# A decoder of 13 blocks on one core: value products moved ahead in the attentions, and a sampling block rewritten

## The reference

```
q, k, v = x @ Wq + bq, ctx @ Wk + bk, ctx @ Wv + bv      # ctx is x itself in self-attention
att = softmax(q @ k.T * scale, masked)                   # 128 x 128 for each sample and head
y   = x + (att @ v) @ Wo + bo
```

```
off  = x @ w_off + b_off                     # two numbers a point
attw = softmax(x @ w_attw + b_attw)          # over the 4 points of a head
ix   = ((clip(off[..., 0], 0, 1) + 1) * L - 1) / 2       # a place between two context rows
hy   = a factor of the other coordinate, 0 to 1
sampled = v[x0] * (1 - frac(ix)) + v[x0 + 1] * frac(ix)  # linear interpolation, v = ctx @ w_value + b_value
out = x + (sum over points of attw * hy * sampled) @ w_out + b_out
```

## Time and profile before

| | |
|---|---|
| runs | 2893.71, 2899.68, 2900.45 us; median 2899.68 |
| profiled execution | 2894.97 us, its span 2893.3 us |
| mean granted clock of PE | 0.934 |
| PE busy | 2543.5 us, 88% of the span |
| DVE busy | 1754.3 us, 61% |
| ACT busy | 1333.5 us, 46% |
| POOL busy | 809.0 us, 28% |

### The profile page before, as it was taken

How to read it: one execution, slowest core, us unless ns; L and a number is a source line. 1 busy time by engine, 2 the same in 40 slices (tenths; PEclk the granted TensorE clock), 3 DMA queues, 4 the chain that set the end, 5 groups by cost and what they waited for, 6 DMA issues and landing times. The chain is left out here.

```text
span 2893.3 us, 48158 instructions
## 1 busy us (share of the span) xinstructions
PE 2543.5 (88%) x15973; PEld 1864.1 (64%) x15973; DVE 1754.3 (61%) x4475; ACT 1333.5 (46%) x3461; POOL 809.0 (28%) x627
## 2 busy tenths in 40 slices
PE   4998989989778789599998998987969889869997
PEld 2666756766555446477776776756965566449996
DVE  7876886589788644344444657874336488434443
ACT  2333664255687513444443445753432388323342
POOL 5533430045100044122211224741110044132222
PEclk8999999999877699799999999988989999989999
DMA  9001000000200144200001002033120120531110
GB/s 320 11 0 50 14 12 9 1 16 1 63 8 1 23 116 118 102 1 1 1 1 41 23 1 74 2 127 105 38 90 6 39 62 5 186 120 50 54 50 26
DMA packets 152054, 142.45 MB, mean 49 GB/s; under 512 B 59948, under 2 KB 136770, under 8 KB 151428
## 3 DMA queue, kind: packets, MB, share of 16 engines
q1 hardware_dynamic: 139668, 110.61, 13.2%
q0 software_dynamic: 10560, 27.19, 2.7%
q10 hardware_dynamic: 1584, 1.57, 0.2%
HBM read 98.14 MB, written 43.02 MB: 49 GB/s over the span
## 5 line engine op out<-in xcount | busy, mean ns | idle before, releaser
L970 POOL TENSOR_TENSOR room<-room 128x1024 f32<-128x1024 f32 x144 | 273.8, 1902 | 414.4 <-DVE room L903 414.3
L1445 PE MATMUL l3f_out<-room,Y 128*128 x624 | 141.0, 380 | 0.0
L897 DVE TENSOR_REDUCE room<-room 128x8 f32<-128x1024 f32 (+1 forms) x144 | 140.0, 972 | 0.8 <-ACT room L1048 0.8
L970 POOL TENSOR_TENSOR room<-room,Y 128x1024 f32<-128x1024 f32 x32 | 60.7, 1896 | 232.6 <-DVE Y L903 232.6
L1445 PEld LDWEIGHTS l3f_out<-room,Y 128*128 128x128 f32 x624 | 115.8, 190 | 14.0
L2488 POOL DMA_INDIRECT sorted_rows<-room,l1f_place_i x32 | 31.0, 967 | 277.7 <-DVE l1f_place_i L2199 268.2
L1046 ACT ACTIVATE room<-l2a_scores,Y 128x128 f32<-128x128 f32 x256 | 71.0, 379 | 75.2 <-DVE Y L889 75.2
L1046 ACT ACTIVATE room<-l1a_scores,room 128x128 f32<-128x128 f32 x256 | 71.4, 386 | 59.6 <-DVE room L889 59.6
L1046 ACT ACTIVATE room<-l0x_scores,room 128x128 f32<-128x128 f32 x256 | 70.5, 384 | 59.0 <-DVE room L889 59.0
L614 PE MATMUL l2a_proj<-room 128*128 128x256 f32 x384 | 93.9, 388 | 0.0
L1747 DVE SCALAR_TENSOR_TENSOR Y<-Y,vecs 128x256 f32<-128x256 f32 x39 | 18.9, 484 | 114.3 <-DMA Y<-out,l3f_dest 114.2
(11 more groups left out here) (832 smaller groups left out, 7062.1 us busy)
## 6 DMA issues: line engine op xcount, KB each, us to landing
sorted_rows<-head SPq DMA_DIRECT2D x1, 16640.0 KB, 57.9
room<-in_L_ffn_w SPq DMA_DIRECT2D x16, 1024.0 KB, 12.9
room<-in_L_ffn_W SPq DMA_DIRECT2D x16, 1024.0 KB, 12.1
Y<-sorted_rows SPq DMA_DIRECT2D x62, 130.0 KB, 2.1
room<-in_ctx SPq DMA_DIRECT2D x24, 256.0 KB, 2.8
room<-sorted_rows SPq DMA_DIRECT2D x39, 130.0 KB, 2.1
room<-results SPq DMA_DIRECT2D x8, 512.0 KB, 7.2
room<-in_L_ffn_routed_w SPq DMA_DIRECT2D x4, 512.0 KB
```

Of the source, the lines that this page charges most:

```text
L897: dve.tensor_reduce(rsum[:, u % 2, 0:SUMMED], p[:, u % (TURN + 1), 0:SUMMED, :], AX.X, ALU.add)
L970: pool.tensor_tensor(p[:, u % (TURN + 1), :, :], p[:, u % (TURN + 1), :, :], rinv[:, u % (TURN + 1), :].unsqueeze(2).to_broadcast([P, HEAD ...
L1445: mm = pe.matmul(obank[n % 2][:, 0:D], hT[:, n % 2, f, :], chip.room[:, bass.ds(at + (SLOT // 2 + f * D), D)], start=(f == 0), stop=(f == ...
```

## The change

Two parts. **In `attention_block`**, so in six blocks, PE issues `values(t-VALUES)` directly behind `score(t)`, ahead of every projection and of the turn of that step; and ACT's copy of the value products moves from behind the evictions of place 1 to directly behind the first exponentials. DVE and POOL keep their order. **`deform_block`** is rewritten. The tent is now made as min(max(v, 0), max(u, 0)), where u and v are two lines already multiplied by the point's weight, with context rows on the partitions (two points at a time: 2 x 64 rows) and the queries of four samples on the free axis. For each of 16 units (4 for each group of samples) and 8 pairs of points, 128 slots in all, PE makes u and v (two bf16 products of 112 x 128 x 512, L3438 and L3439, into one of two PSUM banks each), ACT writes max(u, 0) to W (128 x 512), DVE writes min(max(v, 0), W) back to W (one SCALAR_TENSOR_TENSOR from PSUM, 128 x 512), and PE does four value products from W as it is, with no transposes (L3463), a unit later. The products for slot n+2 wait for `w_ready` of slot n. Context row 63 is handled apart (`edges`, `e63`, `eT`: two products of 128 x 128 x 512 a group). The splitting into bf16 parts (`make_parts`), which now has the weights folded in, is on DVE for the first group and on POOL for the others; the normalisation and the output bias move to POOL. Two weights and a bias are loaded in 16 permuted pieces in place of three, and the context of a group in 6 transfers in place of one.

```diff
@@ attention_block, PE
                 for t in range(T + VALUES + 2):
                     if t < T:
                         score(t)
+                    if 0 <= t - VALUES < T:
+                        values(t - VALUES)
                     for x in at[(t, 0)]:
                         project(x)
                     if 0 <= t - TURN < T:
                         turn(t - TURN)
-                    for x in at[(t, 1)]:
-                        project(x)
-                    if 0 <= t - VALUES < T:
-                        values(t - VALUES)
-                    for x in at[(t, 2)]:
+                    for x in at[(t, 1)] + at[(t, 2)]:
                         project(x)
@@ attention_block, ACT
                         exps(t, 0)
+                    if 0 <= t - VALUES < T:
+                        u = t - VALUES
+                        b, st = divmod(u, S)
+                        act.wait_ge(pv_done, u + 1)
+                        act.copy(oT[:, b % 2, st * CS:(st + 1) * CS, :], out[:, 0:CS * P].rearrange("p (c q) -> p c q", c=CS)).then_inc(out_copied, 1)
                     for x in at[(t, 0)]:
...
-                    if 0 <= t - VALUES < T:
-                        u = t - VALUES
-                        b, st = divmod(u, S)
-                        act.wait_ge(pv_done, u + 1)
-                        act.copy(oT[:, b % 2, st * CS:(st + 1) * CS, :], out[:, 0:CS * P].rearrange("p (c q) -> p c q", c=CS)).then_inc(out_copied, 1)
@@ deform_block, PE
+                def distances(k, p):
+                    n = k * PAIRS_U + p
...
+                    if n >= 2:
+                        pe.wait_ge(w_ready, n - 1)
+                    at = (p % 4 * 4 + p // 4 * 2) * NR
+                    pe.matmul(u_bank[n % 2][:, :], selector[0][0:KS, at:at + P], partsT[0:KS, k % 4, :], start=True, stop=True)
+                    pe.matmul(v_bank[n % 2][:, :], selector[1][0:KS, at:at + P], partsT[0:KS, k % 4, :], start=True, stop=True).then_inc(d_filled, 1)
+                def values(k, i):
...
+                    for e in range(4):
+                        at = o * D + (st * 4 + e) * 32
+                        mm = pe.matmul(o_bank[st][32 * e:32 * e + 32, j * P:(j + 1) * P], v[:, g % 2, j, at:at + 32], W[:, k % 2, tt * 4 + e, j * P:(j + 1) * P],
+                                       start=False, stop=(o == 1 and tt == 1), skip_group_check=True)
+                for k in range(-1, UNITS + 2):
+                    for i in range(PAIRS_U):
+                        if k + 1 < UNITS:
+                            distances(k + 1, i)
+                        if 0 <= k < UNITS:
+                            values(k, i)
+                        for x in tasks_at(k, i):
+                            task(x)
@@ deform_block, DVE
+                def tent(k, p):
+                    n = k * PAIRS_U + p
+                    dve.wait_ge(u_ready, n + 1)
+                    dve.scalar_tensor_tensor(out=W[:, k % 2, p, :], in0=v_bank[n % 2][:, :], scalar=0.0, in1=W[:, k % 2, p, :], op0=ALU.max, op1=ALU.min).then_inc(w_ready, 1)
@@ deform_block, ACT
+                def relu(k, p):
+                    n = k * PAIRS_U + p
+                    if p == 0 and k >= 2:
+                        act.wait_ge(sampled, k - 1)
+                    act.wait_ge(d_filled, n + 1)
+                    act.activation(W[:, k % 2, p, :], u_bank[n % 2][:, :], ACT.Relu).then_inc(u_ready, 1)
```

More of the change, by code:

```diff
@@ L3277, in deform_block @@
-        bank = [chip.ps(f"l1x_bank{i}", scope) if i >= 4 else None for i in range(8)]
-        dist = [chip.ps(f"l1x_dist{i}", scope, 1024) for i in range(2)]
-        w_bank, o_bank, p_bank = bank[4:6], bank[6], bank[7]
+        cT = sb("cT", [P, KC, TG])
+        oT = sb("oT", [P, 2, TG])
+        eT = sb("eT", [P, 2, TG])
+        selector = [half_sb(f"selector{n}", [P, PTS * NR]) for n in range(2)]
+        partsT = half_sb("partsT", [P, 4, TG])
+        parts = half_sb("parts", [P, GR * 4, KS])
@@ new lines, in deform_block, with tasks_at @@
+        OUT_AT = {(0, 3): 0, (0, 6): 1, (1, 1): 2, (1, 5): 3}
+        ADD_AT = {(0, 4): 0, (0, 7): 1, (1, 2): 2, (1, 6): 3}
+        BY_VECTOR = "qvw"
+        opening = [(0, x) for x in (() if first_turned else ("y0", "y1")) + ("q0", "q1", "c0", "c1", "x0", "v0", "v1")] + [(1, "y0"), (1, "y1")] + [(0, f"s{c}") for c in range(4)]
+        def tasks_at(k, i):
+            if (k % 4, i) not in SLOT_OF:
+                return []
+            name, ahead = SLOT_OF[(k % 4, i)]
+            x = (k // 4 + ahead, name)
+            return [x] if x[0] < NG and x not in opening else []
@@ new lines, in deform_block @@
+        turns = opening + [x for k in range(-1, UNITS) for i in range(PAIRS_U) for x in tasks_at(k, i)]
+        rotating = [p_bank, y_bank, o_bank[0], o_bank[1]]
+        bank_of, number, in_front, last_on, emptied_at = {}, {}, {}, {}, {}
+        evicted = {True: 0, False: 0}
+        for n, x in enumerate(turns):
+            place = n % 4 if x in opening else 0
+            bank_of[x], number[x], in_front[x] = rotating[place], n + 1, last_on.get(place)
+            last_on[place] = x
+            evicted[x[1][0] in BY_VECTOR] += 1
+            emptied_at[x] = evicted[x[1][0] in BY_VECTOR]
@@ L3432, in _ @@
-                    if k + 2 < NB:
-                        distances(k + 2, 0)
-                        distances(k + 2, 1)
-                    if 0 <= k - 1 < NB:
-                        sample(k - 1)
-                    if k == NB and head:
-                        pe.wait_ge(d_emptied, 4 * NB)
-                        head.turn(pe, [d[:, 0:512] for d in dist])
+                        if k >= 4 and (k % 4, i) in OUT_AT:
+                            output((k // 4 - 1) * GR + OUT_AT[(k % 4, i)])
@@ new lines, in empty @@
+                def empty(x):
+                    g, name = x
+                    i, bank = int(name[1]), bank_of[x]
+                    wait_filled(act, x)
+                    if name[0] == "y":
+                        op = act.copy(yT[:, i, :], bank[:, :])
+                    elif name[0] == "c":
+                        op = act.copy(cT[:, i, :], bank[:, :])
+                    elif name[0] == "x":
+                        op = act.copy(c63T[:, :, :].rearrange("p c t -> p (c t)"), bank[:, 0:D])
+                    elif name[0] == "s":
+                        op = act.copy(partsT[0:KS, i, :], bank[0:KS, :])
+                    else:
+                        if g == 0:
+                            act.wait_ge(edge_zeroed, 2)
+                        for j in range(GR):
+                            rows = slice(32 * j, 32 * j + 32)
+                            op = act.copy(eT[rows, g % 2, j * P:(j + 1) * P], bank[rows, 0:P])
+                    op.then_inc(p_by_scalar, 1)
@@ new lines, in _ @@
+                for x in opening:
+                    if x == (0, "v0"):
+                        exp(0)
+                    if x[1][0] not in BY_VECTOR:
+                        empty(x)
+                for k in range(-1, UNITS + 2):
+                    for i in range(PAIRS_U):
+                        if k + 1 < UNITS:
+                            relu(k + 1, i)
+                        if i == 0 and k >= 2 and k % 2 == 0:
+                            copy_out((k - 2) // 4, (k - 2) // 2 % 2)
+                        for x in tasks_at(k, i):
+                            if x[1][0] not in BY_VECTOR:
+                                empty(x)
+                        if k % 4 == 0 and i == 5 and k // 4 + 1 < NG:
+                            exp(k // 4 + 1)
+                        if k == UNITS - 2 and i == 7:
+                            act.preload_act_table(ACT.Sqrt)
+                        if k == UNITS - 1 and i == 2 and head:
+                            head.roots(act)
```

640 lines of the change are left out of this document (319 added, 321 removed).

## The result

The changed kernel took 2923.17 us (median of 5 runs, 2913.71 to 2927.22) against 2895.86 before (5 runs, 2888.28 to 2900.45): ratio 1.0091, 95% interval 1.0068 to 1.0113. It is slower by 0.9%, about 26 us. The forecast was +9 in a range up to 2942: the sign and the range held, the size did not.

The account below looks back on a forecast made before the run. Attentions were taken as bound by PE at full clock, l1x by three engines waiting for each other and PE half the time at half speed. Attentions +24 and sampling block -15 gave +9, 2909 us; range 2872 to 2942.

Parts of the forecast that it names:

- Attentions bound by PE, nothing catches up a wait: l1a and l2fa: PE is full at clock 0.99, so every new wait of PE is a loss in full.
- The length of the waits: Value products wait for copies: 2.3 us in l1a's k step; seven four-step groups a block, +10 in l1a, +24 in l2fa.
- Four steps take 20.62 us before, and 20.62 + 2.3 - 0.4 = 22.5 at most after: l1a: a four-step group lengthened by the k step's wait, less savings; 22.1 us was taken.
- the high end of +38: Six attentions: stalls in full, no saving in l2a and l2x, +5 in l3x; the low end was +8.
- rival (c): l1x: clock stays low in much of the new loop; +34 with a quarter of slots, +43 with a third; chance 0.22.
- my 1.25 of 1.44: l1x's loop: PE needs 1.25 us a slot at full clock; 1.44 us a slot taken, 184 us for 128 slots.
- l1x: Sampling block: opening 24.3, loop 184, end 14 and 6 for the clock make 228 us, -15 against 242.9.
- not near any wait: l1x: POOL works beside the other engines without being near any wait; opening only 2 us longer, 24.3.
- the 6 us for the clock: l1x: 6 us added for stretches at the lower clock, each 10 us losing 5 where PE sets the pace.
- The savings of the new order: Attentions: fewer changes of product shape on PE save 3 us in l0x, 6 in l2a and 3 in l2x.
- ACT's part in l2fa: l2fa's y step: exponentials, out copy and y's eviction ahead of ACT's copy make 5.1 us between value products, against 3.97.
- my 0.27 a step: l2fa's y step: the out copy's new place puts 0.27 us more ahead of ACT's copy of the turned probabilities.

Follow-up runs that it names:

- the filler: The changed kernel with six useless bf16 products on PE in each k step's wait of l1a and l2fa: 2904.94 us, ratio to before 1.0043.
- e5_pool_later: The changed kernel with POOL's output-bias additions and second normalisation held back until the first group's parts are made: 2921.34 us, ratio to before 1.0074.
- e3_copy_first: The changed kernel with DVE's copy of the turned probabilities ahead of k's evictions in l1a and l2fa: 2897.42 us, ratio to before 1.0014.
- e9_half_copy: The changed kernel with DVE's copy of the turned probabilities behind four of k's eight evictions in l1a and l2fa: 2908.05 us, ratio to before 1.0012.

## Why the prediction was right and wrong

**Attentions bound by PE, nothing catches up a wait: right.** PE's idle time ahead of L713 is put down to DVE L920, as the prediction said it would be; for the y step in l2fa it names no engine, and the copy L1077 ends just ahead.

**The length of the waits: right, their number not.** 2.3 us forecast in l1a's k step, 2.08 measured. I counted seven groups a block; the traces have six of k's waits in each. With the clock held by the filler the group takes 22.0 us (the starts of its second steps' scores, 659.81 and 681.83 in that kernel) against 22.1 forecast, and the block +10.1 against +10. In l2fa +22.2 against +24. That the blocks fit so well with one group fewer is in part luck: six groups of 1.4 us are 8.4 of l1a's 10.1, and the steps at the block's ends gave the rest.

**The step that failed** is "Four steps take 20.62 us before, and 20.62 + 2.3 - 0.4 = 22.5 at most after", and with it the high end of +38 for the attentions (by its own terms +36, as the low end is +7 and not +8), which the measured +41.5 is above. It priced PE's work around the wait at full clock. I charged a fall of the clock to the sampling block, where before's trace had shown one, as 6 us and as rival (c), and not to the attentions, where PE would still be busy for over 90% of the time. The runs showed the reverse: l1x ran at 0.99 in its loop with short waits spread over its slots (PE busy for 164.75 of 178.90 us, 92%; my 1.25 of 1.44 is 87%), and one wait of 2.0 to 2.5 us in every 22 to 24 us of l1a and l2fa had the clock at 0.50 behind it in nine cases of twelve. The lower clock cost 10.0 us in l1a and 6.6 in l2fa, nearly all of the 17.5 us by which the attentions (+41.5) are above the forecast (+24).

The Trainium skill's rule that I weighed ("TensorE: Matmul & The Clock Gate", A second HAM failure mode: psum-queue depth-cycling) would have had l1x's loop go up and down; the trace does not agree, with 2.6 us of 178.9 at the lower level. What happened in the attentions is nearer to what the Trainium skill describes on the same page under "HAM oscillation — how this bites in real kernels": a pause that comes back in each turn of a loop and lets the clock fall each time. The page's case is a wait for DMA; here it was one for an eviction, and the clock fell in nine of twelve turns.

**l1x: right in sum, not in its terms.** 225.9 against 228. The opening took 30.1, not 24.3 (POOL beside DVE, which I had called "not near any wait"; 7.7 us by `e5_pool_later`), a slot 178.9 / 128 = 1.40, not 1.44, the end 16.9, not 14, and of the 6 us for the clock 1 was needed in this execution. That the sum fits is in good part luck, as these errors cancel. PE's wait ahead of L3438 is for DVE's tent, as forecast:

```profile
L3438 PE MATMUL l1x_u<-room 112*128 112x512 bf16 x128 | 49.9, 390 | 7.2 <-DVE room L3619 6.8
```

**The savings of the new order: right in size where they could be seen.** l2a -6.5 (-6 forecast, a guess by its own words), with PE's busy time down from 348.22 to 343.06 us; l0x -0.2 to -3.7 in different kernels (-3). That the fewer changes of shape are the reason is argued; no run sets them apart. l2x saved nothing, 202.0 to 202.3 us in each kernel with ACT's copy early, and 197.1 in both with that copy late: there the forecast missed that the copy's new place costs the block about 5 us. l3x (+2 forecast) was between -1.1 and +1.6.

**ACT's part in l2fa** was forecast right: 5.1 us for the y step, and 5.02 from one row of value products to the next (1854.94 to 1859.96). Of its terms the eviction of y makes the wait, but taking it out of the way gives back little, as the projection behind needs it; q's eviction, in a step that the forecast had at PE's own pace, made a wait of its own once k's was shorter. What the out copy adds, my 0.27 a step, no run shows.

## What to carry to other kernels

When a change makes TensorE wait in a stretch where it was full, price the wait and then what TensorE does behind it at half clock: here a wait of 2.1 us cost up to 3.8 (0.38 and 1.34 us more in the two rows behind it). If such a wait can't be avoided, useless products in it can be cheaper than an idle engine, as they were here. Before moving a consumer nearer to its producer, look for the longest thing that stands ahead of the producer in each step of the cycle, not in the mean step; one step in four decided in l1a, two in l2fa. And an order that is right for one block can be wrong for its neighbour with the same code, as k in l1a and l2fa is evicted ahead of the copy and in l0x behind it.

## What the runs showed of the hardware

- PE in a stretch at the upper level and over 90% busy fell to 0.50 for 3.4 us behind a single wait of 2.1 us (l1a), and in `e3_copy_first` behind three of six waits of 1.68 us in l2fa. It did not fall in l2fa of `e9_half_copy`, where each group has waits of 0.98, 0.66 and 1.02 us, for 143 us. Nor did it behind each long one: two waits of 1.96 us in l1x's loop left it up, and in l2fa of the changed kernel one of 2.47 us (value products at 1845.10) left it up while the next of 2.46 did not. What decides between them no run shows.
- One DVE TENSOR_TENSOR of 128 x 256 took 1.34 us beside POOL's TENSOR_TENSOR and 0.43 without it. TENSOR_SCALAR, with one input, was slowed as well, from 0.29 to 1.20 us (L3578 in the two kernels):

```profile
789.71 1.20 DVE L3578 TENSOR_SCALAR Y<-Y 128x256 f32<-128x256 f32 x1
```

```profile
790.47 0.29 DVE L3578 TENSOR_SCALAR Y<-Y 128x256 f32<-128x256 f32 x1
```

- The same block l1x with the same code took 225.9, 228.0 or 232.0 us in different kernels. At 225.9 its loop was 178.9 us with 2.2 to 2.6 us at the lower clock, at 232.0 it was 182.0 with 9.9, and the end went with the clock too. The 228.0 of `e3_copy_first` came in the opening (32.2 us), not in the loop. What sets which of them comes was not tested.
